# The causal mask of the max pass: added by VectorE inside the maximum, instead of by 64 mask matmuls per batch

## The chip, the cores and the metric

The kernel runs on one core of one Trainium2 chip. The metric is the device time of one execution, in microseconds; lower is better.

## What is computed

One transformer block, with the layer norms behind the residuals, on 16 batches of 512 tokens with 128 features, in float32. Attention has 16 heads of 8 features.

```python
qkv = hidden_states @ c_attn_w + c_attn_b
scores = jnp.einsum('bhqd,bhkd->bhqk', q, k) / jnp.sqrt(jnp.float32(hd))
scores = jnp.where(causal[None, None], scores, mask_value)
attn = jax.nn.softmax(scores, axis=-1)        # three of the heads are re-weighted by token region
out = jnp.einsum('bhqk,bhkd->bhqd', attn, v)
x = _layernorm(x + out @ c_proj_w + c_proj_b)
x = _layernorm(x + ffn(x))                     # 256 -> 512 -> 512 -> 128, weights +1 or -1
```

The change concerns the maximum over the keys that the softmax subtracts from each row of scores.

## The kernel before

**Two score passes.** For each batch and head, the scores are computed twice. The *max pass* (`max_scores`, L802) computes them with queries on the partitions and keys along the free dimension, in `max_ps`, a ring of three PSUM banks. VectorE reduces each block to its row maximum, negated (`take_max`, L633). Then the maxima are split into three bf16 parts (`split_negmax`), transposed by TensorE (`negmax_transposes`), copied out (`take_negmaxT`, L673), and written by a DMA from ScalarE's queue (`negmax_rows`, L539) into three extra rows of the stacked operand `stack`. The *score pass* (`scores`, L830) computes the scores transposed, with keys on the partitions, and the extra rows subtract the maximum within the matmul. ScalarE takes the exponential of its result (L513), GpSimd zeroes the part above the diagonal (L422), and TensorE sums over the keys (`sums`, L875).

**The mask of the max pass.** In `part` of `max_scores`, one matmul (L816) writes the scores of one head and one query tile of 128, over only the keys that the tile can see: 128, 256, 384 or 512 of them. The last 128 keys are the diagonal block, where half is in the future. A second matmul (L818), `future_bf` against `ident_bf`, adds -3e38 there by accumulation. There are 64 parts per batch, thus 64 mask matmuls.

**The loop.** An iteration n has 4 quarters g of 10 steps t. In every step TensorE issues, in this order: one step of the max pass (of the batch and quarter that `ahead` names, three quarters ahead of the scores: batch n+1 from g=1 on), one step of the score pass of batch n, in the odd steps a quarter of the sums, and then whatever `PLACES` puts at this step: projections, transposes, and the feed-forward matmuls of batches n-1 and n-2. Within a quarter, steps 0 to 3 of the max pass write one block of 512 keys, steps 4 to 7 one of 384 and one of 128, steps 8 and 9 two of 256 (two heads). `take_max` does one `reduce_max` in steps 0 to 3 (L638), two in 4 to 7 (L641, L642), and a single one over both heads in 8 and 9 (L645).

**What sets the order.** Every engine's stream is written by hand and runs in order. A step of the max pass waits until VectorE has taken the block of three steps before (`max_taken`, the ring). A step of the scores waits for the exponential of two steps before. In VectorE's stream, `take_max` comes first in a step, then the bank that `PLACES` gives it (normalising `tok_*`, residual adds with layer norm statistics L702 to L712, `negmaxT`), then the high parts of the feed-forward operands (L717), then the split of the maxima. The two score passes, the feed-forward of two earlier batches and the layer norms thus share each iteration. Iterations run from -2 to 17; the max pass of a batch runs in the iteration before its own.

Of the kernel before, what the change touches and what calls it, by code (L numbers as in the profile page):

```python
# [30 lines left out]
BF16 = mybir.dt.bfloat16  # L31
ALU = mybir.AluOpType
ACT = mybir.ActivationFunctionType
AX = mybir.AxisListType

HEADS = 16
FOCUS = 1.6
EPS = 1e-5
NEG = -3.0e38
# [16 lines left out]
    ("tok_1", -1, (1, 3), (1, 3)),  # L56
    ("negmax1", 0, (1, 4), (1, 4)),
    ("tok_2", -1, (1, 5), (1, 5)),
# [5 lines left out]
    ("x1T", -1, (3, 2), (3, 2)),  # L64
    ("negmax0", 1, (3, 3), (3, 4)),
    ("ffn0_0", -1, (3, 5), (3, 5)),
# [44 lines left out]
def block_kernel(nc, x, w_qkv, b_qkv, w_proj, b_proj, k0, k1, k2, s0, s1, s2, out):  # L111
    B, S, D = x.shape
    H, R = HEADS, D // HEADS
    P = 128
    T = S // P
# [5 lines left out]
    HALF = H // 2  # L121
    MAX_RING = 3
    QK_ROWS, MAX_ROW = 72, 72
# [17 lines left out]
    def use_of(b, what):  # L141

        return use(b + -dict(BANK_USES)[what], what)

    with ExitStack() as ctx:
        def sb(name, shape, dt=F32):
            return ctx.enter_context(nc.sbuf_tensor(name, shape, dt))

        def sem(name):
            return ctx.enter_context(nc.semaphore(name))  # L150
# [8 lines left out]
        ident = sb("ident", [P, P])  # L159
        ident_bf = sb("ident_bf", [P, P], BF16)  # L160
        future_bf = sb("future_bf", [P, P], BF16)
        mult = sb("mult", [P, T, 3])
# [22 lines left out]
        vaug = [sb(f"vaug{i}", [P, T, H, R + 1]) for i in range(2)]  # L185
        negmax = sb("negmax", [P, 2, T, HALF])
        negmax_rest = sb("negmax_rest", [P, 2, T, HALF])
        negmax_parts = sb("negmax_parts", [P, 2, T, 3, HALF], BF16)
        negmaxT = sb("negmaxT", [3 * HALF, 2, S], BF16)
        e = [sb(f"e{i}", [P, STEPS, S]) for i in range(2)]  # L190
# [22 lines left out]
        w0_half = e[0][:, 5, :]  # L213
        ones_bf = e[1][:, 0, :].bitcast(BF16)[0:3, 0:S]

# [16 lines left out]
        max_taken = sem("max_taken")  # L232
        negmax_step = sem("negmax_step")
        negmax_in = [sem(f"negmax_in{i}") for i in range(2)]
        scored = sem("scored")
# [24 lines left out]
        def wait_free(eng, u):  # L260
            eng.wait_ge(bank_free[u[0]], u[1])
# [15 lines left out]
        def _(sp):  # L277
# [21 lines left out]
            for i in range(2):  # L299
                sp.dma_start(stack[i][MAX_ROW:ALL_ROWS, :, 1, :],  # L300
                             ones_bf.unsqueeze(1).broadcast_to([3, H, S])).then_inc(ones_in[i], 16)

# [62 lines left out]
        def _(pool):  # L365

            step = 0
            for t, v in ((ident, 0.0), (ident_bf, 0.0), (future_bf, 0.0), (mult, FOCUS)):
                nc.gpsimd.memset(t[:], v).then_inc(consts_step, 1)
                step += 1  # L370
            nc.gpsimd.memset(minus_half[:], -0.5).then_inc(consts_step, 1)
            nc.gpsimd.memset(one[:], 1.0).then_inc(consts_step, 1)
            nc.gpsimd.memset(ones_bf, 1.0).then_inc(consts_step, 1)
            step += 3
            pool.wait_ge(consts_step, step)
            for t in (ident, ident_bf):
                nc.gpsimd.affine_select(out=t[:], in_=t[:], compare_op=ALU.not_equal, fill=1.0, base=0,
                                        pattern=[[-1, P]], channel_multiplier=1).then_inc(consts_step, 1)
            nc.gpsimd.affine_select(out=future_bf[:], in_=future_bf[:], compare_op=ALU.is_ge, fill=NEG, base=0,
                                    pattern=[[1, P]], channel_multiplier=-1).then_inc(consts_step, 1)  # L380

# [116 lines left out]
        def _(act):  # L498
# [36 lines left out]

            def negmax_rows(b, half):

                wait_free(act, use_of(b, f"negmax{half}"))
                nc.scalar.dma_start(stack[b.parity][MAX_ROW:ALL_ROWS, HALF * half:HALF * half + HALF, 0, :],  # L539
                                    negmaxT[:, half, :]).then_inc(negmax_in[half], 16)  # L540

            def iteration(n):
                for g in range(G):
                    for t in range(STEPS):
                        if live(n):
                            exp(n, g, t)
                        if (g, t) == NEGMAX_ROWS[0] and live(n + 1):
                            negmax_rows(n + 1, 0)
                        if (g, t) == NEGMAX_ROWS[1] and live(n):
                            negmax_rows(n, 1)  # L550
                        for i in range(T):
# [47 lines left out]
        def _(dve):  # L599
# [49 lines left out]
            def split_negmax(b, half, k):  # L649

                m, r = negmax[:, half], negmax_rest[:, half]
                hi, mid, lo = (negmax_parts[:, half, :, i, :] for i in range(3))
                if k:
                    dve.wait_ge(negmax_step, b.times(8, 4 * half + k))
# [10 lines left out]
                ins.then_inc(negmax_step, 1)  # L665

            def take_negmaxT(b, half):
                u = use_of(b, f"negmax{half}")
# [56 lines left out]
            def iteration(n):  # L725
                for g in range(G):
                    for t in range(STEPS):
# [3 lines left out]
                        for what, d, _, step in PLACES:  # L731
                            b = n + d
                            if step != (g, t) or not live(b):
                                continue
                            if what[:6] == "negmax":
                                take_negmaxT(b, int(what[6]))
                            if what == "v":
# [33 lines left out]
                        for k in range(4):  # L771
                            if (g, t) == NEGMAX_SPLIT[0][k] and live(n + 1):
                                split_negmax(n + 1, 0, k)
                            if (g, t) == NEGMAX_SPLIT[1][k] and live(n):
                                split_negmax(n, 1, k)
                        if (g, t) == LN_VAR[0] and live(n + -1):
# [8 lines left out]
        def _(pe):  # L785
# [16 lines left out]
            def max_scores(b, g, t):  # L802
# [27 lines left out]
            def scores(n, g, t):  # L830
# [4 lines left out]
                if t == 0 and g % 2 == 0:  # L835
                    pe.wait_ge(negmax_in[g // 2], n.times(16, 16))
                if not (n.c == 0 and g == 0 and t < 2):
# [42 lines left out]

            def negmax_transposes(b, half):
                u = use_of(b, f"negmax{half}")
                pe.wait_ge(negmax_step, b.times(8, 4 * half + 4))
                bank = claim(u).bitcast(BF16)
                for qt in range(T):
                    last = nc.tensor.transpose(bank[0:3 * HALF, P * qt:P * qt + P],
                                               negmax_parts[:, half, qt].rearrange("p c h -> p (c h)"), ident_bf[:])
                last.then_inc(bank_full[u[0]], 1)
# [36 lines left out]
            def fill_bank(b, what):  # L925
                u = use_of(b, what)
                if what[:6] == "negmax":
                    negmax_transposes(b, int(what[6]))
                if what[:4] == "ffn1":
# [84 lines left out]
```

## Time and profile before

| | us |
|---|---|
| median of 3 runs | 1004.72 |
| lowest, highest | 1001.64, 1010.22 |
| the profiled execution | 1005.2 |
| its span, first to last instruction | 1003.3 |

| engine | busy us | share of the span |
|---|---|---|
| TensorE, matmuls (PE) | 901.3 | 90% |
| TensorE, weight loads (PEld) | 502.5 | 50% |
| VectorE (DVE) | 671.5 | 67% |
| ScalarE (ACT) | 604.2 | 60% |
| GpSimd (POOL) | 438.2 | 44% |

A matmul's busy time contains the latency of its pipeline, so PE at 90% doesn't mean an array that streams 90% of the time; the distance between the starts of two matmuls in a dense run is what one costs. The same holds in part for VectorE, whose operations overlap their ends with the next start.

### The profile page before, as it was taken

What the parts mean: (1) busy time and instruction counts of PE and PEld (TensorE: products, weight loads), DVE (VectorE), ACT (ScalarE), POOL (GpSimd) and SP (SyncE); (2) the same over time, 40 slices, a digit from 0 to 9 for tenths busy, and PEclk for the clock granted to TensorE, in tenths of its full rate; (3) what the DMA queues carried; (4) which work ended last, traced back from release to release, by engine and by line L of the source; (5) the groups of instructions that cost most, each with busy time, mean ns of one, the idle gap of its engine ahead of it and who ended that gap; (6) DMA issues with size and microseconds to landing.
All of it is one profiled execution on the core that took longest, in us unless ns stands there. A gap on an engine that the chain in (4) does not pass through costs nothing.

```text
span 1003.3 us, 18215 instructions
## 1 busy us (share of the span) xinstructions
PE 901.3 (90%) x6848; PEld 502.5 (50%) x6848; DVE 671.5 (67%) x1752; ACT 604.2 (60%) x1106; POOL 438.2 (44%) x505
## 2 busy tenths in 40 slices
PE   2349799999999999999999999999999999999866
PEld 1125344555555554555555554655565554645343
DVE  2255668586877868586877868585867869685334
ACT  2105557576666757576766757576766767476733
POOL 1102334545454554545454554535554554435430
PEclk9657999999999999999999999999999999999887
DMA  3654545345353535445353525454353525300000
GB/s 77 67 68 60 66 54 65 53 61 68 42 68 41 74 39 75 52 63 67 44 66 42 75 40 75 50 65 65 49 64 43 73 30 75 39 23 2 23 10 10
DMA packets 66141, 53.23 MB, mean 53 GB/s; under 512 B 4519, under 2 KB 64007, under 8 KB 66055
## 3 DMA queue, kind: packets, MB, share of 16 engines
q1 hardware_dynamic: 65190, 51.30, 40.2%
q8 instruction: 54, 0.88, 0.4%
q10 hardware_dynamic: 864, 0.79, 0.3%
q14 instruction: 33, 0.26, 0.1%
HBM read 9.24 MB, written 4.19 MB: 13 GB/s over the span
## 4 chain that ended last, share of the span: by engine, by line
PE 63%; ACT 18%; DVE 7%; DMA 5%; issue 2%; SPq 2%; POOL 1%; ACTq 1%; POOLq 0%; DVEq 0%
PE av_ps L875 11%; PE max_ps L816 10%; PE score_ps L842 10%; PE bank_ps L902 7%; PE bank_ps L903 7%; ACT e L513 6%; PE bank_ps L799 4%; ACT res L531 4%; PE max_ps L818 4%; PE bank_ps L948 3%; DVE h_hi L717 3%; ACT full L505 2%; DMA stack<-negmaxT 2%; DMA stack<-parts 2%; PE bank_ps L937 2%
## 5 line engine op out<-in xcount | busy, mean ns | idle before, releaser
L513 ACT ACTIVATE e<-score_ps 128x512 f32<-128x512 f32 x640 | 370.5, 597 | 210.4 <-PE score_ps L842 207.6
L816 PE MATMUL max_ps<-stack 72*128 72x512 bf16 (+3 forms) x1024 | 277.6, 311 | 31.4 <-DMA stack<-parts 24.1
L842 PE MATMUL score_ps<-stack 75*128 75x512 bf16 (+3 forms) x1024 | 247.1, 303 | 24.5 <-DMA stack<-negmaxT 16.7
L638 DVE TENSOR_REDUCE negmax<-max_ps 128x1 f32<-128x512 f32 x256 | 170.2, 684 | 127.9 <-PE max_ps L818 127.6
L422 POOL TENSOR_SCALAR_AFFINE_SELECT e<-e 128x512 f32<-128x512 f32 x256 | 162.8, 656 | 139.2 <-ACT e L513 139.2
L429 POOL TENSOR_TENSOR h_lo<-full,h_hi 128x512 fp32r<-128x512 f32 x120 | 155.1, 1297 | 112.4 <-DVE h_hi L717 112.4
L816 PEld LDWEIGHTS max_ps<-stack 72*128 72x128 bf16 x1024 | 101.8, 99 | 192.0 <-issue 73.4
L818 PE MATMUL max_ps<-ident_bf,future_bf 128*128 128x128 bf16 x1024 | 197.4, 224 | 0.0
L875 PE MATMUL av_ps<-e,vaug 128*9 128x512 f32 (+3 forms) x2048 | 187.4, 438 | 2.1 <-ACT avT L520 1.9
L641 DVE TENSOR_REDUCE negmax<-max_ps 128x1 f32<-128x384 f32 x256 | 140.3, 548 | 47.4 <-PE max_ps L818 47.0
L505 ACT ACTIVATE full<-bank_ps,scales 128x512 f32<-128x512 f32 x128 | 86.6, 688 | 99.9 <-PE bank_ps L903 97.0
L842 PEld LDWEIGHTS score_ps<-stack 75*128 75x128 bf16 x1024 | 85.3, 99 | 71.5 <-ACT e L513 21.9
L717 DVE CAST h_hi<-full 128x512 fp32r<-128x512 f32 x128 | 78.8, 616 | 63.3 <-ACT full L505 62.1
L818 PEld LDWEIGHTS max_ps<-ident_bf,future_bf 128*128 128x128 bf16 x1024 | 103.0, 101 | 17.1 <-issue 12.3
L902 PE MATMUL bank_ps<-h_hi,w 128*128 128x512 f32 x256 | 105.5, 412 | 0.5 <-DVE h_lo L722 0.3
L645 DVE TENSOR_REDUCE negmax<-max_ps 128x2 f32<-128x512 f32 x128 | 84.6, 683 | 27.2 <-PE max_ps L818 27.1
L903 PE MATMUL bank_ps<-h_lo,w 128*128 128x512 f32 x256 | 101.1, 395 | 0.0
L434 POOL TENSOR_TENSOR rstd<-var_eps,minus_half 128x4 f32<-128x4 f32 x32 | 32.5, 1015 | 154.0 <-DVE var_eps L712 154.0
L405 POOL TENSOR_TENSOR qk<-qk,parts 128x1024 f32<-128x1024 f32 x15 | 31.9, 2127 | 133.5 <-ACT qk L505 133.5
L642 DVE TENSOR_REDUCE negmax<-max_ps 128x1 f32<-128x128 f32 x256 | 71.2, 278 | 0.0
L875 PEld LDWEIGHTS av_ps<-e,vaug 128*9 128x9 f32 x2048 | 31.0, 88 | 65.7 <-issue 61.1
L531 ACT ACTIVATE res<-res,shift,rstd 128x128 f32<-128x128 f32 x128 | 52.6, 488 | 8.1 <-POOL shift L437 8.1
(86 smaller groups left out, 945.8 us busy)
## 6 DMA issues: line engine op xcount, KB each, us to landing
stack<-parts SPq DMA_DIRECT2D x288, 128.0 KB
x_in<-in_L_attn_hidden_states SPq DMA_DIRECT2D x16, 256.0 KB, 4.8
x_res<-in_L_attn_hidden_states SPq DMA_DIRECT2D x16, 256.0 KB, 11.0
out_x<-res SPq DMA_DIRECT2D x16, 256.0 KB, 10.3
stack<-negmaxT ACTq DMA_DIRECT2D x32, 24.0 KB
e<-in_L_ffn_k SPq DMA_DIRECT2D x1, 256.0 KB, 3.1
wc<-in_L_attn_c_attn_w SPq DMA_DIRECT2D x1, 192.0 KB
e<-in_L_ffn_k SPq DMA_DIRECT2D x1, 128.0 KB, 3.2
```

Source lines behind the costliest of these rows:

```text
L422: last = nc.gpsimd.affine_select(out=ap, in_=ap, compare_op=ALU.is_ge, fill=0.0, base=0, pattern=[[0, 4], [1, P]], channel_multiplier=-1)
L429: nc.gpsimd.tensor_tensor(h_lo[layer][:, m, :], full[:, full_slot(b, k), :], h_hi[layer][:, m, :].bitcast(F32), ALU.subtract).then_inc(spl ...
L513: nc.scalar.activation(e[g % 2][:, t, :], score_ps[:, t % 2, :], ACT.Exp, scale=SCALE).then_inc(exped, 1)
L638: ins = nc.vector.reduce_max(negmax[:, half, 3, h + t:h + t + 1], buf, AX.X, negate=True)
L641: nc.vector.reduce_max(negmax[:, half, 2, i:i + 1], buf[:, 0:3 * P], AX.X, negate=True)
L717: nc.vector.tensor_copy(hi, full[:, full_slot(b, k), :]).then_inc(hi_ready, 1)
L816: nc.tensor.matmul(out_ap[:, col:col + width], st[0:QK_ROWS, h, 0, P * qt:P * qt + P], st[0:QK_ROWS, h, 1, 0:width], start=True, stop=False)
L818: return nc.tensor.matmul(out_ap[:, col + width - P:col + width], future_bf[:], ident_bf[:], start=False, stop=True)
L842: return nc.tensor.matmul(out_ap[:, col:col + width], st[0:ALL_ROWS, h, 1, P * kt:P * kt + P], st[0:ALL_ROWS, h, 0, P * kt:S], start=True, ...
L875: last = nc.tensor.matmul(av_ps[32 * j:32 * j + R + 1, P * kt:S], vaug[b.parity][:, kt, G * g + j, :], src, start=(order == 0), stop=(orde ...
L902: nc.tensor.matmul(bank, w, hi, start=(i == 0), stop=False)
L903: last = nc.tensor.matmul(bank, w, lo, start=False, stop=(i == len(pairs) - 1))
```

## The change

VectorE adds the mask while it takes the maximum, by one `tensor_tensor_reduce` per block. That operation reads the block from PSUM and a bf16 tile `future` of 512 columns from SBUF (zeros, with the -3e38 triangle in the last 128), writes the sum back over the block in PSUM, and writes the row maximum to its accumulator output. The mask matmuls go. Since the maxima are now not negated, the constant rows that they meet in the matmul become -1. In steps 8 and 9 there are now two operations, one for each head, in place of one. The buffer of the transposed maxima is one half where it was two, with waits that follow from it. Everything named `negmax` becomes `rowmax`.

```diff
-            for t, v in ((ident, 0.0), (ident_bf, 0.0), (future_bf, 0.0), (mult, FOCUS)):
+            for t, v in ((ident, 0.0), (ident_bf, 0.0), (future, 0.0), (mult, FOCUS)):
...
-            nc.gpsimd.memset(ones_bf, 1.0).then_inc(consts_step, 1)
+            nc.gpsimd.memset(minus_ones, -1.0).then_inc(consts_step, 1)
...
+                def masked_max(qt, i, col):
+                    scored_block = buf[:, col:col + P * (qt + 1)]
+                    return nc.vector.tensor_tensor_reduce(
+                        out=scored_block, in0=scored_block, in1=future[:, P * (T - 1 - qt):S], scale=1.0, scalar=NEG,
+                        op0=ALU.add, op1=ALU.max, accum_out=rowmax[:, half, qt, i:i + 1])
+
                 if t < 4:
-                    ins = nc.vector.reduce_max(negmax[:, half, 3, h + t:h + t + 1], buf, AX.X, negate=True)
+                    ins = masked_max(3, h + t, 0)
                 elif t < 8:
-                    i = h + t - 4
-                    nc.vector.reduce_max(negmax[:, half, 2, i:i + 1], buf[:, 0:3 * P], AX.X, negate=True)
-                    ins = nc.vector.reduce_max(negmax[:, half, 0, i:i + 1], buf[:, 3 * P:S], AX.X, negate=True)
+                    masked_max(2, h + t - 4, 0)
+                    ins = masked_max(0, h + t - 4, 3 * P)
                 else:
-                    i = h + 2 * (t - 8)
-                    ins = nc.vector.reduce_max(negmax[:, half, 1, i:i + 2],
-                                               buf.rearrange("p (h k) -> p h k", h=2), AX.X, negate=True)
+                    masked_max(1, h + 2 * (t - 8), 0)
+                    ins = masked_max(1, h + 2 * (t - 8) + 1, 2 * P)
                 ins.then_inc(max_taken, 1)
...
-                if b.c > 0:
-                    dve.wait_ge(negmax_in[half], b.times(16))
+                if half:
+                    dve.wait_ge(rowmax_in[0], b.times(16, 16))
+                elif b.c > 0:
+                    dve.wait_ge(rowmax_in[1], b.times(16))
                 src = bank_ps[0:3 * HALF, u[0], :].bitcast(BF16)[:, 0:S]
-                nc.vector.tensor_copy(negmaxT[:, half, :], src).then_inc(bank_free[u[0]], 1)
+                nc.vector.tensor_copy(rowmaxT[:], src).then_inc(bank_free[u[0]], 1)
...
-                    nc.tensor.matmul(out_ap[:, col:col + width], st[0:QK_ROWS, h, 0, P * qt:P * qt + P],
-                                     st[0:QK_ROWS, h, 1, 0:width], start=True, stop=False)
-                    return nc.tensor.matmul(out_ap[:, col + width - P:col + width], future_bf[:], ident_bf[:],
-                                            start=False, stop=True)
+                    return nc.tensor.matmul(out_ap[:, col:col + width], st[0:QK_ROWS, h, 0, P * qt:P * qt + P],
+                                            st[0:QK_ROWS, h, 1, 0:width], start=True, stop=True)
```

## Rows read from the trace of the kernel before

**Rows 1.** The page: busy time of each engine; shares of the chain that ended last.

```profile
PE 901.3 (90%) x6848; PEld 502.5 (50%) x6848; DVE 671.5 (67%) x1752; ACT 604.2 (60%) x1106; POOL 438.2 (44%) x505
...
PE 63%; ACT 18%; DVE 7%; DMA 5%; issue 2%; SPq 2%; POOL 1%; ACTq 1%; POOLq 0%; DVEq 0%
```

**Rows 2.** Windows: length, busy us (count) of PE, PEld, DVE, ACT, POOL; clock, DMA, GB/s.

```profile
90.00:146.00 56.00, 47.48 (x393) 22.05 (x392) 33.40 (x82) 32.80 (x59) 16.88 (x20) 0.94 0.50 62
...
539.50:595.70 56.20, 54.55 (x430) 30.66 (x429) 41.16 (x109) 37.46 (x69) 27.99 (x32) 1.00 0.42 58
...
933.00:1003.00 70.00, 46.37 (x237) 26.90 (x235) 26.32 (x80) 30.08 (x57) 21.72 (x25) 0.83 0.06 15
```

**Rows 3.** Groups by line and shape: count, busy us, mean ns, idle before, releaser.

```profile
L818 PE MATMUL max_ps<-ident_bf,future_bf 128*128 128x128 bf16 x1024 | 197.4, 224 | 0.0
L638 DVE TENSOR_REDUCE negmax<-max_ps 128x1 f32<-128x512 f32 x256 | 170.2, 684 | 127.9 <-PE max_ps L818 127.6
L641 DVE TENSOR_REDUCE negmax<-max_ps 128x1 f32<-128x384 f32 x256 | 140.3, 548 | 47.4 <-PE max_ps L818 47.0
...
L642 DVE TENSOR_REDUCE negmax<-max_ps 128x1 f32<-128x128 f32 x256 | 71.2, 278 | 0.0
...
L722 DVE TENSOR_TENSOR x_lo<-full,x_hi 128x512 fp32r<-128x512 f32 x16 | 16.8, 1048 | 0.5
...
L754 DVE TENSOR_TENSOR res<-bank_ps,x_res 128x512 f32<-128x512 f32 x16 | 10.9, 683 | 2.3 <-PE bank_ps L960 2.2
```

**Rows 4.** The chain that ended last, in order of time: start, us, what.

```profile
500.61 1.54 ACT res L531 x4
...
513.37 0.06 PE max_ps L818
```

**Rows 5.** Timeline of PE: start, duration, line and operation, [idle before, releaser].

```profile
498.53 0.38 PE L816 MATMUL max_ps<-stack 72*128 72x512 bf16 x1 [0.24 <-DVE negmax L642]
...
513.62 0.39 PE L816 MATMUL max_ps<-stack 72*128 72x512 bf16 x1
```

**Rows 6.** Windows of L818 alone: length, busy us (count) of PE and PEld.

```profile
485.20:491.36 6.16, 1.27 (x6) 0.59 (x6) 1.00 0.27 41
...
513.60:516.00 2.40, 0.56 (x3) 0.29 (x3) 1.00 0.59 61
516.00:535.50 19.50, 2.67 (x14) 1.38 (x14) 1.00 0.56 59
```

**Rows 7.** Windows of VectorE alone: length, busy us (count).

```profile
491.30:506.30 15.00, 14.45 (x47) 1.00 0.67 76
507.80:513.60 5.80, 5.61 (x12) 1.00 0.37 75
516.00:535.50 19.50, 9.36 (x25) 1.00 0.56 59
```

**Rows 8.** Windows of VectorE's reads of max_ps alone: length, busy us (count).

```profile
491.30:506.30 15.00, 8.23 (x18) 1.00 0.67 76
507.80:513.60 5.80, 3.40 (x8) 1.00 0.37 75
```

**Rows 9.** Timeline of VectorE within one iteration.

```profile
494.00 0.17 DVE L711 TENSOR_SCALAR neg_mean<-moments 128x4 f32<-128x4 f32 x1
494.08 0.16 DVE L712 TENSOR_SCALAR var_eps<-moments 128x4 f32<-128x4 f32 x1
...
503.16 0.69 DVE L638 TENSOR_REDUCE negmax<-max_ps 128x1 f32<-128x512 f32 x1 [0.25 <-PE max_ps L818]
...
505.91 0.40 DVE L673 COPY negmaxT<-bank_ps 24x512 bf16<-24x512 bf16 x1
...
507.90 0.43 DVE L717 CAST h_hi<-full 128x512 fp32r<-128x512 f32 x1 [0.92 <-ACT full L505]
...
512.88 2.47 DVE L638 TENSOR_REDUCE negmax<-max_ps 128x1 f32<-128x512 f32 x4
```

**Rows 10.** Timeline of ScalarE behind the take of the transposed maxima.

```profile
507.18 1.27 ACT L505 ACTIVATE full<-bank_ps,scales 128x512 f32<-128x512 f32 x2 [1.01 <-PE bank_ps L903]
```

More of the change, by code:

```diff
@@ L56 @@
     ("tok_1", -1, (1, 3), (1, 3)),
-    ("negmax1", 0, (1, 4), (1, 4)),
+    ("rowmax1", 0, (1, 4), (1, 4)),
     ("tok_2", -1, (1, 5), (1, 5)),
@@ L64 @@
     ("x1T", -1, (3, 2), (3, 2)),
-    ("negmax0", 1, (3, 3), (3, 4)),
+    ("rowmax0", 1, (3, 3), (3, 4)),
     ("ffn0_0", -1, (3, 5), (3, 5)),
@@ L160, in block_kernel @@
         ident_bf = sb("ident_bf", [P, P], BF16)
-        future_bf = sb("future_bf", [P, P], BF16)
+        future = sb("future", [P, S], BF16)
         mult = sb("mult", [P, T, 3])
@@ L185, in block_kernel @@
         vaug = [sb(f"vaug{i}", [P, T, H, R + 1]) for i in range(2)]
[L186 to L189, printed above, removed]
+        rowmax = sb("rowmax", [P, 2, T, HALF])
+        rowmax_rest = sb("rowmax_rest", [P, 2, T, HALF])
+        rowmax_parts = sb("rowmax_parts", [P, 2, T, 3, HALF], BF16)
+        rowmaxT = sb("rowmaxT", [3 * HALF, S], BF16)
         e = [sb(f"e{i}", [P, STEPS, S]) for i in range(2)]
@@ L232, in block_kernel @@
         max_taken = sem("max_taken")
-        negmax_step = sem("negmax_step")
-        negmax_in = [sem(f"negmax_in{i}") for i in range(2)]
+        rowmax_step = sem("rowmax_step")
+        rowmax_in = [sem(f"rowmax_in{i}") for i in range(2)]
         scored = sem("scored")
@@ L378, in _ @@
                                         pattern=[[-1, P]], channel_multiplier=1).then_inc(consts_step, 1)
-            nc.gpsimd.affine_select(out=future_bf[:], in_=future_bf[:], compare_op=ALU.is_ge, fill=NEG, base=0,
-                                    pattern=[[1, P]], channel_multiplier=-1).then_inc(consts_step, 1)
+            latest = future[:, S - P:S]
+            nc.gpsimd.affine_select(out=latest, in_=latest, compare_op=ALU.is_ge, fill=NEG, base=0,
+                                    pattern=[[-1, P]], channel_multiplier=1).then_inc(consts_step, 1)
             first_end = max(1, S // 3)
@@ L534, in layernorm_out, with rowmax_rows @@
                     ins.then_inc(ln_step[i], 1)
-            def negmax_rows(b, half):
-                wait_free(act, use_of(b, f"negmax{half}"))
+            def rowmax_rows(b, half):
+                wait_free(act, use_of(b, f"rowmax{half}"))
                 nc.scalar.dma_start(stack[b.parity][MAX_ROW:ALL_ROWS, HALF * half:HALF * half + HALF, 0, :],
-                                    negmaxT[:, half, :]).then_inc(negmax_in[half], 16)
+                                    rowmaxT[:]).then_inc(rowmax_in[half], 16)
             def iteration(n):
@@ L636, in take_max, with split_rowmax @@
                 dve.wait_ge(max_scored, b.times(G * STEPS, STEPS * g + t + 1))
+                def masked_max(qt, i, col):
[3 more added lines that the diff above has]
+                        op0=ALU.add, op1=ALU.max, accum_out=rowmax[:, half, qt, i:i + 1])
                 if t < 4:
[L638 removed]
+                    ins = masked_max(3, h + t, 0)
                 elif t < 8:
[L640 to L646 removed]
+                    masked_max(2, h + t - 4, 0)
+                    ins = masked_max(0, h + t - 4, 3 * P)
+                else:
+                    masked_max(1, h + 2 * (t - 8), 0)
+                    ins = masked_max(1, h + 2 * (t - 8) + 1, 2 * P)
                 ins.then_inc(max_taken, 1)
[L649 to L652 removed]
+            def split_rowmax(b, half, k):
+                m, r = rowmax[:, half], rowmax_rest[:, half]
+                hi, mid, lo = (rowmax_parts[:, half, :, i, :] for i in range(3))
                 if k:
[L654 removed]
+                    dve.wait_ge(rowmax_step, b.times(8, 4 * half + k))
                 else:
@@ L734, in iteration @@
                                 continue
-                            if what[:6] == "negmax":
-                                take_negmaxT(b, int(what[6]))
+                            if what[:6] == "rowmax":
+                                take_rowmaxT(b, int(what[6]))
                             if what == "v":
@@ L835, in scores @@
                 if t == 0 and g % 2 == 0:
-                    pe.wait_ge(negmax_in[g // 2], n.times(16, 16))
+                    pe.wait_ge(rowmax_in[g // 2], n.times(16, 16))
                 if not (n.c == 0 and g == 0 and t < 2):
@@ L879, in sums, with rowmax_transposes @@
                     last.then_inc(summed, 1)
-            def negmax_transposes(b, half):
-                u = use_of(b, f"negmax{half}")
-                pe.wait_ge(negmax_step, b.times(8, 4 * half + 4))
+            def rowmax_transposes(b, half):
+                u = use_of(b, f"rowmax{half}")
+                pe.wait_ge(rowmax_step, b.times(8, 4 * half + 4))
                 bank = claim(u).bitcast(BF16)
@@ L886, in negmax_transposes @@
                     last = nc.tensor.transpose(bank[0:3 * HALF, P * qt:P * qt + P],
-                                               negmax_parts[:, half, qt].rearrange("p c h -> p (c h)"), ident_bf[:])
+                                               rowmax_parts[:, half, qt].rearrange("p c h -> p (c h)"), ident_bf[:])
                 last.then_inc(bank_full[u[0]], 1)
@@ L926, in fill_bank @@
                 u = use_of(b, what)
-                if what[:6] == "negmax":
-                    negmax_transposes(b, int(what[6]))
+                if what[:6] == "rowmax":
+                    rowmax_transposes(b, int(what[6]))
                 if what[:4] == "ffn1":
```

18 lines of the change are left out of this document (9 added, 9 removed).

## Prediction

> **What bounds the kernel now.** I read the page first. TensorE is busy for 90% of the span and holds 63% of the chain that ended last; ScalarE holds 18%, VectorE 7% though it is busy for 67% [rows 1]. By that, work taken from TensorE and given to VectorE should pay. The shares are averages, so next came the windows of one iteration each. From 202 to 877 us the rows repeat almost to the digit: 56.2 us per iteration, PE 54.6, VectorE 41.2, ScalarE 37.5, full clock [rows 2]. The time is thus about twelve of these, a first one (90 to 146) with less work, a start of 90 us, and a last stretch of 70 us that has no max pass.
>
> Within one iteration the load of VectorE is very uneven, and this decides the case. From 516 to 535.5 us, where TensorE runs the feed-forward matmuls, it is busy 9.36 of 19.5 us; from 491.3 to 506.3 it is busy 14.45 of 15.0, and from 507.8 to 513.6 5.61 of 5.8 [rows 7]. There the layer norm statistics, the residual adds and the high parts fall between the takes of the maximum. TensorE feels it: at 498.53 a step of the max pass waits 0.24 us for L642, through the ring of three [rows 5]. At 513.62 a step starts 0.05 us after the end (512.88 + 0.69) of the first of four L638 [rows 5, 9], the take whose bank it needs. No wait is noted there, but there is no slack either. In the dense stretch ScalarE is on the chain too (four L531 at 500.61 [rows 4]), so VectorE is not the longest there, only next to it.
>
> **What goes from TensorE.** The row says 224 ns for a mask matmul [rows 3], but that is its latency; on the chain one takes 0.06 us [rows 4], 0.058 by the distance of starts in dense runs. 64 are 3.7 us per iteration, some 7% of 56.2. That would be the whole gain if TensorE set the pace throughout. It does so in the lightly loaded part only: after 513.62 there are 3 and 14 masks up to 535.5, and in the shape of the next iteration 6 more from 485.2 to 491.4 [rows 6]. Of the 14, one lies beside a wait for ScalarE's copy of xT. So 22 masks count: 22 x 0.058 = 1.27 us per iteration. The weight loads of the masks (0.10 us each) overlap matmuls today and are priced at nothing; if they don't overlap, the gain is larger, not smaller.
>
> **What comes to VectorE.** A block of 512 is 684 ns as a reduction from PSUM, and an add with one operand in PSUM and one in SBUF is 683 [rows 3]: the second operand and the 512 outputs cost nothing there. That the outputs go to PSUM here, in place, no row shows; I take it as free by L754. In a dense run the four L638 take 2.47 us, so one costs (2.47 - 0.69) / 3 = 0.593 and overlaps the rest. By the rows of 512 and 128 an element costs (684 - 278) / 384 = 1.06 ns [rows 3], so 0.05 of the 0.593 is fixed, and up to 0.07 by the other shapes; I take 0.07. Steps 8 and 9 pay this fixed part once more: 8 x 0.07 = 0.56 us per iteration.
>
> The unknown is x, what the accumulator output adds to each of the 64 operations. No row of before has one. Below: nothing, if the value leaves with the operation, as in TENSOR_REDUCE. Above: the operation must end in full before a small one reads the accumulator out, 0.684 + 0.163 - 0.593 = 0.25 us [rows 3, 9]. Between: one more small instruction in the stream. The nearest rows are L711 and L712, of four elements, whose starts are 0.08 us apart [rows 9]. I take x = 0.08, since an instruction behind another in order is what that row shows.
>
> The Trainium skill, "VectorE: DVE Perf Modes", section "Two Vector instructions with no wait between them", says that an operation that also gives out its accumulator is two instructions, the main one and a read of the accumulator; no row of before shows one. "Vector Engine (DVE) Microarchitecture Reference", 5.2, gives about 75 ns per instruction once they overlap, against the 80 of the row. By these pages x would be 0.075, an estimate, and the sum below 2 us lower; they speak against x = 0.
>
> A second doubt is the port that VectorE shares with GpSimd. L722, with two inputs in SBUF, averages 1048 ns for 512 columns; L754, with one, stays at 683 [rows 3]. The new operation has one input in SBUF, so I price contention at nothing; if it did contend like L722, a block of 512 would cost 0.36 us more beside a GpSimd busy for 44%, 0.16 on average, the same as x = 0.24.
>
> **The sum over one iteration.** Where does the dense stretch move? TensorE brings the takes forward by 1.27 us, less two operations (2x) in front of an earlier L673 that ScalarE waits for in order. From 491.3 to L673 at 505.91 VectorE is full. It has 18 reads of max_ps, one of which starts behind L673, and two are L645 [rows 8]: 17 + 2 = 19 operations, so + 19x + 0.14, less the idle 0.25 at 503.16 [rows 9]. L673 sets the next work: it frees the bank of a feed-forward matmul, and ScalarE's DMA and its `full` at 507.18 queue behind it [rows 10], for which L717 at 507.90 waits [rows 9]. So the idle 0.92 there moves along and absorbs nothing. From there to the take that TensorE needs at 513.62: two pairs, two L645 (now four) and one L638, 9x + 0.14. In all
>
> -1.27 + 2x + 19x + 0.14 - 0.25 + 9x + 0.14 = -1.24 + 30x us per iteration.
>
> With x = 0.08 this is +1.16 us; it is zero at x = 0.041. At x = 0 the idle 0.25 isn't used up, since TensorE's writes move too (0.06 of it): -1.05. At 0.25, +6.3. The 28 masks that fall in the dense stretch buy nothing in the first case: they make TensorE wait longer for the ring.
>
> **The ends.** The first iteration (90 to 146) has VectorE at 33.4 of 56 [rows 2], so TensorE sets it: some 43 masks on the path, -2.5 us. In the start, where the clock is the lower one, I count some 15 masks on the path, at twice 0.058 roughly -1.6, against +0.4 for five operations in front of the first L673; the rest waits for DMAs. Last 70 us: unchanged. Take 13 full iterations (the twelve, and the one at either end that is nearly so, for 12 plus a half each). Sum: 13 x 1.16 - 2.5 - 1.2 = +11.4 us, on 1005.2 for this execution, which stands 0.5 above the median: 1016.
>
> Nothing for the rest. The memset of `future` is four times as wide (by some 0.4 us), while the engines wait for the weights' DMAs until 9 us. The single buffer of the transposed maxima adds a wait for a DMA issued 20 steps of 40 earlier, half an iteration or 28 us; if it were late, L673 and all behind it would be. The parts 1 and -1 cost the same.
>
> **The rivals.** (1) *The accumulator comes free* (x under 0.03), and TensorE sets the pace: 13 x (-1.05) - 3.7 = -17, 987 to 988 us; up to 998 at x = 0.03. For it: 63% of the chain is PE's, and TENSOR_REDUCE gives its value at no extra cost. Against: an elementwise output of 512 and a single value are two outputs. It decides on the other side, below x = 0.04. Chance 0.25. (2) *In between*, x from 0.03 to 0.07: the gain in the light part is given back in the dense part, 998 to 1013. 0.25. (3) *My forecast*: x from 0.07 to 0.12, VectorE becomes the engine that sets the dense stretch: 1013 to 1035. 0.3. (4) *The read is not overlapped* or the in-place write or the shared port costs as much (x from 0.16 to 0.25): 13 x 3.6 - 2 = +45, 1050, to 13 x 6.3 + 4 = +86, 1091. For it: L722 shows how a VectorE operation can lose half. Against: L754. 0.2.
>
> **How the numbers follow.** 1016 us is the likeliest; its own range is 1010 to 1035. For 8 in 10: 985 leaves out little below, 1062 cuts the upper half of (4). Three runs of before spread over 8.6 us, so that about 1% is what can be told from no change. Faster by over 1% is most of (1): 0.24. Within 1%, from 995 to 1015, is (2) and edges of (1) and (3): 0.28. Slower: 0.48.
>
> **What would show it.** Right: the new operations stand at 0.66 to 0.69 us for 512, with a second row or a gap of 0.08 behind each; VectorE at about 41.2 + 0.56 + 64 x 0.08 = 46.9 us per iteration of 57.4; TensorE's waits for VectorE, at the step of 498.53 0.24 us, become over 1 us; and the chain carries much more of VectorE than 7%. Wrong: VectorE per iteration at 42, iterations of 55.2 (rival 1); a block of 512 at 0.85 or more (rival 4). The account fails too if the wait at 513.62 or the one behind L673 isn't where the delay passes on, or if the clock in the iterations falls from 1.00 because TensorE idles more.

## The result, and the profile after

The kernel with the change took 1016.66 us (median of 19 runs, 1008.17 to 1022.29); the kernel before, run beside it, 1006.41 us (19 runs, 1001.64 to 1010.44). The ratio is 1.0089, with a 95% interval of 1.0067 to 1.0110: slower by 0.9%, some 9 us. The forecast was 1016. The number was met; the sections below show that its terms were not all met, and that two errors of opposite sign cancelled by chance.

The profiled execution of after took 1010.2 us, its span 1008.3 us, against 1005.2 and 1003.3 of before. It is one of the shorter ones of after, so its total says less than its stretches do.

From the page of the kernel after: instructions, busy times, and shares of the chain that ended last (to be read beside [rows 1]).

```profile
span 1008.3 us, 17320 instructions
...
PE 869.5 (86%) x5824; PEld 433.8 (43%) x5824; DVE 728.9 (72%) x2904; ACT 604.3 (60%) x1106; POOL 435.8 (43%) x505
...
PE 49%; DVE 29%; ACT 9%; DMA 5%; issue 4%; SPq 2%; ACTq 2%; POOL 0%; POOLq 0%; DVEq 0%
```

TensorE has 1024 instructions less and 32 us less busy time, VectorE 1152 more and 57 us more. VectorE's share of the chain went from 7% to 29%.

From the groups by line and shape of the kernel after, VectorE (beside [rows 3]): count, busy us, mean ns, idle before, releaser.

```profile
L641 DVE CUSTOM_DVE_ANT_0 max_ps<-max_ps,future 128x512 f32<-128x512 f32 x256 | 175.8, 706 | 106.3 <-PE max_ps L824 104.3
L641 DVE CUSTOM_DVE_ANT_0 max_ps<-max_ps,future 128x384 f32<-128x384 f32 x256 | 144.7, 565 | 35.7 <-PE max_ps L824 35.5
L641 DVE DVE_READ_ACCUMULATOR2_ANT rowmax<- 128x1 f32 x1024 | 142.1, 139 | 0.0
L641 DVE CUSTOM_DVE_ANT_0 max_ps<-max_ps,future 128x256 f32<-128x256 f32 x256 | 103.1, 454 | 15.4 <-PE max_ps L824 14.9
L641 DVE CUSTOM_DVE_ANT_0 max_ps<-max_ps,future 128x128 f32<-128x128 f32 x256 | 84.2, 329 | 0.0
```

Each masked maximum is two rows: the operation, and behind it a read of the accumulator, 1024 of them. The Trainium skill, "VectorE: DVE Perf Modes", section "Two Vector instructions with no wait between them", says just this; the trace agrees. The main operation is on average 22 ns longer than the reduction it replaced for 512 elements (706 against 684), 17 for 384 and 51 for 128.

What the pair costs in the stream, the timeline of VectorE in the kernel after shows (start, duration, line and operation).

```profile
456.04 0.96 DVE L725 CAST h_hi<-full 128x512 fp32r<-128x512 f32 x2
456.93 0.69 DVE L641 CUSTOM_DVE_ANT_0 max_ps<-max_ps,future 128x512 f32<-128x512 f32 x1
457.54 0.14 DVE L641 DVE_READ_ACCUMULATOR2_ANT rowmax<- 128x1 f32 x1
457.54 0.73 DVE L641 CUSTOM_DVE_ANT_0 max_ps<-max_ps,future 128x512 f32<-128x512 f32 x1
458.19 0.14 DVE L641 DVE_READ_ACCUMULATOR2_ANT rowmax<- 128x1 f32 x1
```

The read begins together with the next operation, so its 0.14 us lies beside it. What is left of x depends on what stands in front. From start to start the first block of 512, behind a cast, takes 0.61 us; the second, directly behind a masked maximum, takes 0.65. The reductions of before took 0.60 to 0.61 in either place. The other shapes do the same (medians over the trace): 384 elements take 0.48 behind another kind of operation and 0.52 behind a masked maximum, against 0.47 before; 128, always behind a masked maximum, 0.25 against 0.20; 256 take 0.35 and 0.38. So x is 0.01 us behind another kind of operation and 0.05 directly behind a masked maximum, not 0.08. The Trainium skill, "Vector Engine (DVE) Microarchitecture Reference", 5.2, which the prediction named, gives about 75 ns per overlapped instruction; the measured 10 and 50 are less.

The windows of one iteration each, from one take of the transposed maxima (L673 before, L681 after) to the same take of the next iteration: first one of before, then four of after (beside [rows 2]: length, busy us and count of PE, PEld, DVE, ACT, POOL; clock, DMA share, GB/s).

```profile
482.39:538.64 56.25, 54.69 (x430) 30.81 (x428) 41.25 (x109) 37.46 (x69) 28.07 (x32) 1.00 0.49 58
```

```profile
481.93:538.68 56.75, 52.93 (x366) 26.59 (x364) 44.94 (x183) 37.57 (x69) 27.83 (x32) 0.97 0.46 58
538.68:594.71 56.03, 51.61 (x366) 26.29 (x364) 44.76 (x181) 37.40 (x69) 27.81 (x32) 1.00 0.48 58
651.49:710.85 59.36, 55.35 (x366) 28.39 (x364) 45.18 (x183) 38.14 (x69) 28.32 (x32) 0.91 0.43 55
710.85:768.64 57.79, 54.21 (x366) 27.11 (x364) 44.60 (x183) 37.72 (x69) 28.35 (x32) 0.94 0.47 56
```

Two things are to be seen. VectorE has about 45 us per full iteration, where it had 41.25. And the granted clock, 1.00 in every full iteration of before, is 0.91 to 0.97 in seven of the eleven of after. Before, an iteration takes 56.28 us (the mean of eleven; the prediction's windows said 56.2). After, it takes 56.04 us where the clock holds, in four of the eleven, and that is 0.24 less than before; 56.8 with the clock at 0.97; 57.8 at 0.94; 59.4 at 0.91. Up to 651 us iterations of 56.0 and 56.8 take turns, and behind it come 59.4, 57.8 and 56.8.

Where the clock falls, the timeline of PE in the kernel after shows, with the windows of the same stretch below it. The first half is the timeline (in brackets: idle before, releaser), the second the windows of 1.5 us (busy us and count of PE; clock, DMA share, GB/s).

```profile
272.56 0.38 PE L824 MATMUL max_ps<-stack 72*128 72x512 bf16 x1 [1.36 <-DVE rowmax L641]
272.77 0.38 PE L848 MATMUL score_ps<-stack 75*128 75x512 bf16 x1
273.75 0.39 PE L824 MATMUL max_ps<-stack 72*128 72x512 bf16 x1 [0.60 <-DVE rowmax L641]
```

```profile
270.40:271.90 1.50, 0.80 (x8) 1.00 0.57 64
271.90:273.40 1.50, 0.59 (x2) 1.00 0.75 104
273.40:274.90 1.50, 1.15 (x6) 0.79 1.14 169
274.90:276.40 1.50, 1.50 (x9) 0.50 0.79 76
276.40:277.90 1.50, 1.50 (x7) 0.57 0.57 53
277.90:279.40 1.50, 1.50 (x16) 1.00 0.63 73
```

This is the step that waited 0.24 us for VectorE before [rows 5]; now it waits 1.36 us, and the next one 0.60. TensorE is busy for 1.39 of 3.0 us (0.80 + 0.59), and right behind it the clock falls from 1.00 (2.4 GHz) to 0.50 (1.2 GHz) for some 3.5 us, in which the engine is busy throughout. In the iteration of 59.4 us the same two waits have a longer fall behind them: the first wait ends at 667.69, and the rows below (PE, PEld, DVE, ACT, POOL; clock) show half the clock for ten microseconds.

```profile
668.00:670.00 2.00, 1.40 (x12) 0.23 (x10) 2.00 (x10) 1.46 (x4) 1.78 (x4) 1.00 1.03 171
670.00:672.00 2.00, 2.00 (x14) 0.96 (x7) 1.97 (x8) 1.99 (x5) 1.18 (x3) 0.55 0.82 74
672.00:680.00 8.00, 8.00 (x39) 3.55 (x39) 4.78 (x18) 3.73 (x7) 1.25 (x2) 0.50 0.48 71
```

The four iterations at full clock have the same waits of 1.36 and 0.60 us, with no fall behind them. Where it falls, TensorE becomes late for VectorE as well: between 502 and 504 us, in a fall, VectorE waits 0.23 and 0.32 us for it; in the same stretch of an iteration at full clock it doesn't wait.

### The profile page after: what moved, and what is told of

Read it like the earlier page. It is cut to its first block, busy times and chain, and to the rows that moved or that the text cites. A ratio compares the mean times of both kernels' runs of the same rounds, so it can differ in the third digit from the quotient of the medians.

```text
span 1008.3 us, 17320 instructions
## 1 busy us (share of the span) xinstructions
PE 869.5 (86%) x5824; PEld 433.8 (43%) x5824; DVE 728.9 (72%) x2904; ACT 604.3 (60%) x1106; POOL 435.8 (43%) x505
## 4 chain that ended last, share of the span: by engine, by line
PE 49%; DVE 29%; ACT 9%; DMA 5%; issue 4%; SPq 2%; ACTq 2%; POOL 0%; POOLq 0%; DVEq 0%
DVE max_ps L641 13%; PE av_ps L881 9%; PE max_ps L824 8%; PE score_ps L848 7%; PE bank_ps L908 6%; PE bank_ps L909 6%; DVE h_hi L725 5%; PE bank_ps L954 3%; PE bank_ps L807 3%; DVE stats L710 3%; DVE rowmax L641 2%; ACT e L514 2%; DMA stack<-parts 2%; DMA stack<-rowmaxT 2%; ACT full L506 2%
## 5 line engine op out<-in xcount | busy, mean ns | idle before, releaser
L641 DVE CUSTOM_DVE_ANT_0 max_ps<-max_ps,future 128x512 f32<-128x512 f32 (+3 forms) x1024 | 478.1, 514 | 157.4 <-PE max_ps L824 154.7
L824 PE MATMUL max_ps<-stack 72*128 72x512 bf16 (+3 forms) x1024 | 259.2, 316 | 67.3 <-DVE rowmax L641 39.3
L848 PE MATMUL score_ps<-stack 75*128 75x512 bf16 (+3 forms) x1024 | 252.7, 309 | 24.2 <-DMA stack<-rowmaxT 14.6
L881 PE MATMUL av_ps<-e,vaug 128*9 128x512 f32 (+3 forms) x2048 | 198.8, 462 | 1.9 <-ACT avT L521 1.7
L824 PEld LDWEIGHTS max_ps<-stack 72*128 72x128 bf16 x1024 | 82.5, 100 | 241.5 <-DVE rowmax L641 108.2
L641 DVE DVE_READ_ACCUMULATOR2_ANT rowmax<- 128x1 f32 x1024 | 142.1, 139 | 0.0
L725 DVE CAST h_hi<-full 128x512 fp32r<-128x512 f32 x128 | 77.1, 611 | 58.4 <-ACT full L506 58.4
L908 PEld LDWEIGHTS bank_ps<-h_hi,w 128*128 128x128 f32 x256 | 48.4, 189 | 15.1 <-issue 1.9
L909 PEld LDWEIGHTS bank_ps<-h_lo,w 128*128 128x128 f32 x256 | 48.5, 189 | 9.1
L807 PE MATMUL bank_ps<-ident,avT 128*128 128x128 f32 x256 | 40.7, 282 | 6.7 <-DVE rowmaxT L681 3.4
L954 PE MATMUL bank_ps<-xT,wqk 128*128 128x512 f32 x64 | 39.0, 697 | 3.3 <-ACT xT L506 3.3
```

Source lines behind the costliest of these rows:

```text
L641: return nc.vector.tensor_tensor_reduce(out=scored_block, in0=scored_block, in1=future[:, P * (T - 1 - qt):S], scale=1.0, scalar=NEG, op0= ...
L725: nc.vector.tensor_copy(hi, full[:, full_slot(b, k), :]).then_inc(hi_ready, 1)
L807: last = nc.tensor.transpose(bank[:, P * i:P * i + P], src, ident[:])
L824: return nc.tensor.matmul(out_ap[:, col:col + width], st[0:QK_ROWS, h, 0, P * qt:P * qt + P], st[0:QK_ROWS, h, 1, 0:width], start=True, st ...
L848: return nc.tensor.matmul(out_ap[:, col:col + width], st[0:ALL_ROWS, h, 1, P * kt:P * kt + P], st[0:ALL_ROWS, h, 0, P * kt:S], start=True, ...
L881: last = nc.tensor.matmul(av_ps[32 * j:32 * j + R + 1, P * kt:S], vaug[b.parity][:, kt, G * g + j, :], src, start=(order == 0), stop=(orde ...
```

## The experiments

Each edit is on the kernel after. Ratios are to the kernel before, run beside it on the same chip.

**The kernel after once more.** No edit.

> The changed kernel unchanged, beside the kernel before on the same chip. Theory A (VectorE sets the dense stretch, and TensorE's waits there of 1.4 and 0.6 us also bring its granted clock down now and then): 1.008 to 1.012 of before, mean clock 0.91 to 0.93. It is the scale for the other three.

Measured 1014.73 us (10 runs, 1007.03 to 1024.02) against 1005.87; ratio 1.0081, 1.0053 to 1.0108. The loss is there again, and so is the scatter. Its profiled execution took 1024.0 us, the longest of all 29 of this kernel, with the lowest mean clock, 0.901; the shortest, 1007.0, had the highest, 0.935. Its eleven full iterations took 636.2 us, those of the profiled execution after 625.1; eleven at full clock would be 616.4.

**Half of the change, the added half.** A mask matmul behind every step of the max pass again, over a part of `future` that holds zeros, so that TensorE has its old work and VectorE its new.

```
-    return nc.tensor.matmul(..., start=True, stop=True)
+    nc.tensor.matmul(..., start=True, stop=False)
+    return nc.tensor.matmul(out_ap[:, col + width - P:col + width], ident_bf[:], future[:, 0:P],
+                            start=False, stop=True)
```

> The changed kernel with 64 matmuls per batch put back behind the score matmuls, which add zeros (the mask itself stays with VectorE). It is the added half of the change alone. Theory A: an iteration is about 30 x 0.05 = 1.5 us longer than before, 13 x 1.5 = +20 us, and TensorE idles less, so the clock is up again: 1.018 to 1.026 of before, clock 0.93 to 0.95. Rival B (VectorE's part is hidden and the time of the changed kernel is the fallen clock only): 1.000 to 1.006.

Measured 1030.58 us, ratio 1.0237, 1.0208 to 1.0265. VectorE's new work costs 2.4% when nothing is taken from TensorE. A window of one iteration of this kernel:

```profile
521.74:579.03 57.29, 54.89 (x429) 30.70 (x428) 44.42 (x181) 37.60 (x69) 28.07 (x31) 1.00 0.45 56
```

The iteration at full clock is 57.3 us, 1.0 more than before; those with a fall of the clock, eight of eleven, took 58.1. Part of the 2.4% is thus the clock here too, and TensorE's two waits are only 0.64 and 0.52 us in this kernel.

**The other half alone.** No mask matmuls, and the maximum by the plain reduction of before, one operation in steps 8 and 9. The mask is left out of the max pass altogether, so the maximum takes in the future keys of the diagonal block.

```
-    ins = masked_max(3, h + t, 0)
+    ins = nc.vector.reduce_max(rowmax[:, half, 3, h + t:h + t + 1], buf, AX.X)
...
```

> The removed half alone: no mask in the max pass at all, and plain reductions of positive maxima. The maximum then includes future keys of the diagonal block; the softmax subtracts a value at least as large. Theory A: x = 0, so 13 x (-1.05) - 3.7 = -17 us, 0.980 to 0.986 of before; its wait at the first step of the last quarter is 0.8 us against 0.24 before and 1.4 in the changed kernel, so the clock may fall a little, which costs up to 5 us of it. Rival B: 0.98 too, so this run tells only whether TensorE's part is sized right (if the pace were set by TensorE everywhere, 13 x 3.7 = -48 us, 0.952).

Measured 990.58 us, ratio 0.9821, 0.9789 to 0.9852. So the halves are -1.8% and +2.4%, and their sum of +0.6% lies near the +0.8 and +0.9 of the whole. The waits for VectorE are smaller here (0.96 and 0.47 us), but the clock still falls in its profile (0.94 and 0.97 in turn in the iterations); this profiled execution, 1008.8 us, was the longest of five.

**The clock alone.** Throwaway matmuls of 512 columns, whose results nothing reads, in the two places where TensorE waits: five ahead of step 0 of the last quarter and two ahead of step 1, into a bank that is overwritten afterwards. They add work and take none away.

```
+    if (g, t) in ((3, 0), (3, 1)) and live(n + -1):
+        bank = claim(use_of(n + -1, "x1T"))
+        for _ in range(5 if t == 0 else 2):
+            nc.tensor.matmul(bank, ident_bf[:], future[:], start=True, stop=True)
```

> The changed kernel with 5 and 2 matmuls of 512 columns, whose results are overwritten, ahead of the two steps at which TensorE waits 1.4 and 0.6 us for VectorE: 1.08 and 0.43 us of work inside the waits. Theory A: the granted clock of the iterations is 1.00 again, the mean 0.945 or more, and the time falls to 1.000 to 1.004 of before. Rival C (the dips of the clock have nothing to do with these waits): clock 0.91 to 0.93 and 1.008 to 1.014.

Measured 996.95 us, ratio 0.9918, 0.9889 to 0.9947. The direction is as expected, the gain larger: with seven matmuls more per iteration the kernel is 1.6 to 1.7% faster than after, and now faster than before. In the timeline of PE of this kernel:

```profile
436.61 1.24 PE L985 MATMUL bank_ps<-future,ident_bf 128*128 128x512 bf16 x5
438.13 0.38 PE L824 MATMUL max_ps<-stack 72*128 72x512 bf16 x1 [0.28 <-DVE rowmax L641]
438.34 0.38 PE L848 MATMUL score_ps<-stack 75*128 75x512 bf16 x1
438.56 0.59 PE L985 MATMUL bank_ps<-future,ident_bf 128*128 128x512 bf16 x2
439.32 0.39 PE L824 MATMUL max_ps<-stack 72*128 72x512 bf16 x1 [0.17 <-DVE rowmax L641]
```

The waits of 1.36 and 0.60 us are now 0.28 and 0.17; the step itself comes when VectorE lets it, as before. A window of an iteration of this kernel has the full clock, and so have all others but the first:

```profile
482.00:538.00 56.00, 53.08 (x373) 26.90 (x372) 44.72 (x181) 37.38 (x69) 27.76 (x32) 1.00 0.48 58
```

An iteration is 56.04 us, against 56.0 to 59.4 in after. It is the same as an iteration of after at full clock, so the filling changes nothing else: it takes away the falls. A repeat of this kernel on another chip:

> e3 once more, on this chip, as the base of e8 and as a repeat: 0.988 to 0.996 of before, clock 0.945 or more (theory A), 1.00 to 1.014 if e3's result was a chance of the chip.

Measured 1001.48 us (8 runs), ratio 0.9943, 0.9919 to 0.9967; iterations of 56.04 us again. Both intervals lie below 1. They overlap, so the size is 0.6 to 0.8%, and the way from it to the kernel after is 1.4 to 1.7%, 14 to 17 us. The two profiled executions differ by 8 us in the span, all of it in the first iteration, which takes 49.2 us in the one and 57.3 in the other; from 90 to 146 us the clock is 0.82 and 0.76. Why it is so is open.

**Is it the place, or more matmuls anywhere?** The same seven matmuls at a step where TensorE doesn't wait.

```
-    if (g, t) in ((3, 0), (3, 1)) and live(n + -1):
+    if (g, t) == (0, 4) and live(n + -2):
```

> The changed kernel with the same 7 matmuls of 512 columns, put at step (0, 4), in the light part, where TensorE waits for nothing. Control for e3. Theory A: they cost 7 x 0.215 = 1.5 us in each of 16 iterations, +24 us over the changed kernel, and the waits of the dense part and the dips stay or shrink a little, as TensorE arrives as early as before (the takes are late by the same 1.5 us): 1.022 to 1.034 of before, clock 0.91 to 0.93. Rival F (more work of TensorE anywhere raises the clock and pays for itself): 0.992 to 1.000.

Measured 1044.85 us, ratio 1.0392, 1.0350 to 1.0433. The matmuls do no good there. TensorE's waits for VectorE are those of after, and the clock falls as in after or deeper:

```profile
PE max_ps L824 <- DVE rowmax L641: 38.0, 68, 2.0
```

The kernel after has 39.3 us in 71 waits in that row (total, times, longest), the one filled in the right place 17.1 us in 68. The loss is larger than expected. Two windows of this kernel, of one iteration each, tell why:

```profile
555.24:612.79 57.55, 53.11 (x373) 26.98 (x371) 44.87 (x181) 37.41 (x69) 27.85 (x32) 1.00 0.46 57
612.79:674.83 62.04, 58.16 (x373) 29.19 (x371) 45.38 (x183) 38.30 (x69) 28.40 (x32) 0.89 0.40 53
```

At full clock an iteration is 57.55 us, 1.51 more than in after, just what seven matmuls cost at 0.215 us from start to start, by the row of five above: (1.24 - 0.38) / 4. The rest is the clock: the eleven full iterations took 650.1 us, of which 17 are the matmuls and another 17 the falls, where after lost 9 to the falls in its profiled execution. So this run shows that more matmuls don't help by themselves. Why the falls are deeper here is open.

**The same without the accumulator.** The second experiment with four and one matmuls in the same two places. The mask is left out of the max pass, as there.

> Plain maxima without any mask, and the waits filled by 4 and 1 matmuls of 512 columns. e2 without the dips of the clock: theory A says 56.25 - 1.05 = 55.2 us per iteration at clock 1.00, 0.972 to 0.979 of before. Rival C (dips unrelated): as e2, 0.982, with the clock near 0.92.

Measured 982.32 us, ratio 0.9778, 0.9729 to 0.9827. An iteration is 54.92 us at full clock. It differs from the filled kernel above in the masked maximum (with the second operation of steps 8 and 9), and in two throwaway matmuls fewer: 56.04 - 54.92 = 1.12 us per iteration is what VectorE's new work costs while the clock holds.

**The change in the light part only.** The masked maximum where TensorE sets the pace, the mask matmul and the plain reduction elsewhere. The profile has 512 reads of the accumulator in 16 batches, so it is 32 of the 64 blocks, and not the 28 that the expectation counts.

```
+    light = (g == 3 and t >= 4) or g == 0 or (g == 1 and t < 4)
...
```

> The change in the light part of the iteration only: VectorE masks in quarters 0 and in steps 4 to 9 of quarter 3 and 0 to 3 of quarter 1 of the max pass (28 of 64 blocks); elsewhere the mask matmuls and plain reductions of the kernel before. Theory A (the light part keeps 22 x 0.058 = 1.27 us, the dense part is set by VectorE and gets nothing more to do): -1.2 us per iteration, 13 x -1.2 = -15 us, 0.982 to 0.989 of before; clock as in before or a little under it, since the wait in the dense part stays near 0.3 us. Rival D (what VectorE gets costs the same wherever it is put, and TensorE gains the same wherever it is relieved): 28/64 of the changed kernel's +0.8%, 1.003 to 1.004.

Measured 993.80 us, ratio 0.9871, 0.9820 to 0.9922. An iteration is 55.18 us at the full clock:

```profile
339.01:394.20 55.19, 53.05 (x397) 28.58 (x396) 43.37 (x145) 37.52 (x69) 28.10 (x31) 1.00 0.47 58
```

That is 1.1 us less than before, from half of the blocks. It computes what the reference asks, and it beats both kernels. The prediction's split into a light and a dense part is thus shown: what is moved in the one pays, what is moved in the other costs.

**How much does one more small instruction cost?** On the filled kernel, a copy of four elements ahead of each masked maximum.

```
+    slot = 2 * ((STEPS * g + t) % 14) + (col > 0)
+    nc.vector.tensor_copy(spare[:, slot, :], minus_half[:])
```

> The kernel that fills the waits, with a copy of 4 elements ahead of each of the 64 masked maxima. One such copy costs VectorE 0.07 to 0.08 us in the stream. Theory A (30 of the 64 operations lie on the path of an iteration): 30 x 0.075 = 2.25 us per iteration, 13 x 2.25 = +29 us over e3's 0.992, thus 1.018 to 1.026 of before. Rival E (VectorE is not on the path once the clock is restored): within 5 us of e3, 0.992 to 0.997; and if all 64 counted, 16 x 64 x 0.075 = +77 us, 1.068.

Measured 1124.82 us, ratio 1.1195, 1.1152 to 1.1238: far off. The group of the copy, and the timeline of the engines about one of them, in this kernel:

```profile
L642 DVE COPY spare<-minus_half 128x4 f32<-128x4 f32 x1024 | 303.7, 297 | 111.1 <-PE max_ps L827 109.9
```

```profile
288.17 0.16 DVE L642 COPY spare<-minus_half 128x4 f32<-128x4 f32 x1
...
288.53 0.64 POOL L424 TENSOR_SCALAR_AFFINE_SELECT e<-e 128x512 f32<-128x512 f32 x1 [1.05 <-ACT e L515]
...
288.59 0.61 DVE L642 COPY spare<-minus_half 128x4 f32<-128x4 f32 x1
```

The first copy takes 0.16 us; the second, issued while GpSimd works, ends when GpSimd does (289.20 against 289.17). The median copy took 165 ns and the longest 2067. It was the wrong probe, since it brought a wait for GpSimd of its own. The Trainium skill, "SBUF — State Buffer", section "Who interferes with whom", says that a VectorE operation in a two-port mode is shut out for the whole of a GpSimd instruction that was issued first. The trace agrees as far as the copy's end goes; that the copy ran in such a mode, no run shows. The masked maxima beside it were not held up (690 ns for 512).

**The same question with a reduction.** A maximum over four elements in place of the copy.

```
+    nc.vector.reduce_max(spare[:, slot, 0:1], minus_half[:], AX.X)
```

> As e5, but the small operation is a reduction of 4 elements instead of a copy: in e5 the copies stood still while GpSimd worked (mean 297 ns at a median of 165), so that run added some 0.2 us per operation, not 0.075. A TENSOR_REDUCE showed no such stops in any run so far. If theory A's count of 30 operations on the path holds: +2.25 us per iteration over e9, +29 us, 1.018 to 1.026 of before. If the count is nearer to 17, as the iterations of e3 (56.06 us) and e6 (54.93 us) suggest for an accumulator read of 0.05 us: +1.3 us, +17 us, 1.006 to 1.012. Rival E (the count of e5's loss was right and contention had no part in it): above 1.08.

Measured 1010.56 us (10 runs), ratio 1.0038, 1.0014 to 1.0062; its neighbour on the same chip is the repeat of the filled kernel, 0.9943. An iteration grew from 56.04 to 56.66 us, by 0.62, where 2.25 or 1.3 was expected; the ratio lies below both ranges too. In the timeline of VectorE of this kernel:

```profile
437.78 0.14 DVE L644 DVE_READ_ACCUMULATOR2_ANT rowmax<- 128x1 f32 x1
437.78 0.15 DVE L642 TENSOR_REDUCE spare<-minus_half 128x1 f32<-128x4 f32 x1
437.85 0.69 DVE L644 CUSTOM_DVE_ANT_0 max_ps<-max_ps,future 128x512 f32<-128x512 f32 x1
438.46 0.14 DVE L644 DVE_READ_ACCUMULATOR2_ANT rowmax<- 128x1 f32 x1
```

The small operation takes 0.07 us up to the start of the next, and a block of 512 with it takes 0.68 us (437.78 to 438.46). That is 0.03 more than the 0.65 of one directly behind another masked maximum, and 0.06 more than the 0.61 of one behind another kind of operation. The main operation behind the probe is shorter: 686 ns for 706, 419 for 454 with 256 elements. If 30 operations are on the path, 18 of the first kind and 12 of the second (counted below), this makes 1.3 us per iteration, less some 0.2 of VectorE's idle time that it uses up (0.12 ahead of the dense stretch, 0.09 behind L681). Measured are 0.62. So the probe doesn't confirm the count, and why it cost half as much is open.

## Why the prediction came true, and where it did not

**Right: which engine sets which stretch.** The light part alone gave -1.1 us per iteration (55.18 against 56.28). The removed half gave -1.36 (54.92, with the waits filled). The formula gives -1.33 for it: the prediction's -1.05 for x = 0 contains 0.28 for the second operation of steps 8 and 9, which these kernels don't have, though the expectations took -1.05. The added half alone cost 1.0 (57.29). The step named as the sign waits 1.36 us in place of 0.24, and the step of 513.62 again starts right behind the take it needs: 0.11 us after its end (457.73 against 456.93 + 0.69), 0.05 before. VectorE's share of the chain rose from 7 to 29%, and the second row behind each operation is there.

**Right: no contention and a cheap write in place.** The masked maxima stand at 706 ns, 22 above the reduction. Rival 4, with 0.85 us and more, is out. How x divides between the longer main operation and the read wasn't tried.

**Wrong: the size of x.** The prediction took 0.08 us for each operation, by the distance of two small ones. Measured are 0.01 behind another kind of operation and 0.05 directly behind a masked maximum. Of the 30 on its path, counted in the timeline of the iteration that starts at 425.89 us, 12 stand as the first and 18 as the second, so the mean is 0.034. By the prediction's own cases this is rival 2, "in between", with 998 to 1013 us. The term was 30 x 0.046 x 13 = 17.9 us too high. With 0.034 the prediction's formula gives -1.24 + 30 x 0.034 = -0.22 us per iteration, and measured at full clock are 56.04 - 56.28 = -0.24. The added half checks too: 1.02 + 0.28 less 0.19 of idle time used up is 1.11, measured 1.12. Stretch by stretch it fits less well: from the take at 491.36 to L673 VectorE's stretch grew by 0.71 us where this formula gives 0.52, and from L717 at 507.90 to the first L638 by 0.15 where it gives 0.47. The idle ahead of L717, said to absorb nothing, went from 0.9 to 0.8. In the second the casts L725 are shorter than L717 was (0.96 against 1.21 us for two), and why is open. With the ends the change is worth 13 x (-0.22) - 3.7 = -6.6 us while the clock holds; the two filled runs, whose iterations are those of after at full clock, measured -9 and -4.

**Wrong: the clock, priced at nothing.** The prediction named the wait of over 1 us as a sign and a falling clock as what would upset the account. It gave no price to the link between them. In after, each iteration has waits of 1.36 and 0.60 us close together, and behind them half the clock for 3.5 to some 10 us in seven of eleven. A fall costs 0.7, 1.8 or 3.3 us. Over the eleven iterations this is 9 us in the profiled execution and 20 in that of the repeat. Filling the waits took it away; the same matmuls elsewhere didn't. By the medians it is worth 14 to 17 us.

Put together: the forecast of +11.4 us, less 17.9 for x, plus 14 to 17 for the clock, is +7.5 to +10.5; measured are +9 to +10. So the number was right by luck: the missing term was about as large as the one that was too high. Without the falls of the clock the kernel would have been faster than before, on the other side of the forecast. The direction hung on a term that the sum left out.

Open remains why the same waits cost 3.5 us of half clock in some iterations, 10 in others and nothing in a third kind.

## What to carry to other kernels

Price moved work by the stretch, not by the share of the span: ask for each stretch which engine sets it, and move only the pieces whose receiver has slack there; here 32 of 64 blocks moved gave -1.3%, all 64 gave +0.9%. Where a change makes TensorE wait longer in a kernel that runs at full clock, price the clock as well. Pairs of waits of 1.36 and 0.60, 0.96 and 0.47, and 0.64 and 0.52 us had falls behind them here; the kernel whose longest regular wait for VectorE was 0.63 us (the probe with a reduction) and the one with 0.26 (the light part only) had none in their full iterations. Look at the clock in short windows behind the wait, and try a few throwaway matmuls in the wait itself. Put a probe for a small cost through an operation that can't wait for another engine, and look at the distance of starts, not at durations.

## What the runs showed of the hardware that was not expected

- Behind waits of 1.36 and 0.60 us the granted clock fell from 1.00 to 0.50 for 3.5 to some 10 us in seven of eleven iterations. Matmuls whose result is thrown away, put into the waits, kept it at 1.00 and made the kernel 14 to 17 us faster.
- The read of the accumulator has a row of 139 ns and is nearly hidden: a fused operation of 512 and its read take 0.61 us from start to start behind another kind of operation and 0.65 directly behind another fused one; the plain reduction 0.60 to 0.61.
- A fused operation of 128 elements is 329 ns behind another fused one and 286 behind a small one; of 256, 462 behind another fused one and 419 behind a small one. Between two fused operations an added small one of 0.07 us costs only about 0.03.
- A copy of four elements took up to 2067 ns beside a working GpSimd, a reduction of four elements 149 ns on average.
